# Which rows of x a chunk takes: runs of 1 KB against runs of 6 to 7 KB, and a strided read in VectorE's transposes

## The reference

```python
mask = adj > 0
head = mask.astype(adj.dtype)
head = head / jnp.maximum(jnp.sqrt(jnp.sum(head * head, axis=-1, keepdims=True)), 1e-12)
inc = adj + head                      # each positive entry gains 1 / sqrt(count of positives in its row)
edge_fea = inc @ x
edge_degree = jnp.sum(inc, axis=-1, keepdims=True)
out = layernorm(x + edge_fea / edge_degree)
```

## Time and profile before

| | us |
|---|---|
| median of 3 runs | 430.42 |
| lowest and highest | 429.62, 434.88 |
| the execution that was profiled | 431.71 |
| its span, first to last instruction | 429.9 |
| TensorE busy (matmuls) | 396.9 |
| VectorE busy | 371.7 |
| GpSimd busy | 351.1 |
| ScalarE busy | 346.5 |

### The profile page before, as it was taken

The page is one execution under the profiler, slowest core; times in us unless marked ns, Lnnn a source line. Parts: engine busy times, 40 slices in busy tenths (PEclk is TensorE's granted clock), DMA queues, the critical chain, the costliest instruction groups (busy, mean ns, idle before and its releaser), DMA issues.

```text
span 429.9 us, 8836 instructions
## 1 busy us (share of the span) xinstructions
PE 396.9 (92%) x2152; PEld 344.8 (80%) x2152; DVE 371.7 (86%) x739; ACT 346.5 (81%) x450; POOL 351.1 (82%) x266
## 2 busy tenths in 40 slices
PE   1199767999999999999999999999999999999995
PEld 0177646888888888888888888888888888888884
DVE  0859489899999999999999999999999999999932
ACT  5766799888899889898889988888988999896200
POOL 3108069899999999999999999999999999999850
PEclk9999888999999999999999999999999999999999
DMA  8999857666656666766666666676666666660010
GB/s 233 270 240 263 242 147 220 199 189 194 197 186 199 187 202 207 220 199 192 196 187 196 191 194 197 205 219 202 192 195 194 189 196 189 196 205 24 26 38 12
DMA packets 38219, 79.85 MB, mean 186 GB/s; under 512 B 9536, under 2 KB 21824, under 8 KB 38208
## 3 DMA queue, kind: packets, MB, share of 16 engines
q1 hardware_dynamic: 37824, 78.68, 62.4%
q10 hardware_dynamic: 384, 1.05, 0.8%
HBM read 75.50 MB, written 4.19 MB: 185 GB/s over the span
## 4 chain that ended last, share of the span: by engine, by line
PE 84%; SPq 5%; issue 4%; POOL 2%; DMA 2%; DVE 1%; POOLq 0%
PE edge L618 41%; PE edge L577 21%; PE edge L621 21%; SPq L187 3%; SPq L157 2%; DMA x_stage<-in_x_dram 2%; POOL inc_split L344 2%; PE sums L572 1%; SPq L182 0%; POOL inc_split L349 0%; DVE incT L436 0%; POOL rstd L328 0%; POOLq L45 0%; DVE rows L463 0%; DVE rows L467 0%
## 5 line engine op out<-in xcount | busy, mean ns | idle before, releaser
L618 PE MATMUL edge<-x_split,inc_split 128*128 128x512 f32 (+1 forms) x810 | 281.4, 396 | 0.1
L344 POOL TENSOR_TENSOR inc_split<-incT,inc_split 128x832 fp32r<-128x832 f32 x120 | 237.2, 1987 | 10.5 <-DVE incT L436 7.6
L621 PE MATMUL edge<-x_split,inc_split 128*128 128x256 f32 x780 | 218.3, 280 | 0.0
L618 PEld LDWEIGHTS edge<-x_split,inc_split 128*128 128x128 f32 x810 | 152.9, 189 | 34.9 <-POOL inc_split L344 0.6
L220 ACT ACTIVATE sign_out<-raw,sign_bias 128x1024 bf16<-128x1024 f32 x128 | 146.4, 1144 | 32.4 <-DMA raw<-in_adj_dram 30.9
L420 DVE SCALAR_TENSOR_TENSOR inc<-raw,scaled 128x1024 f32<-128x1024 f32 x128 | 153.5, 1199 | 5.4 <-ACT scaled L231 5.4
L436 DVE STREAM_TRANSPOSE incT<-inc 128x1024 f32<-128x1024 f32 x128 | 155.4, 1225 | 0.2
L231 ACT ACTIVATE scaled<-raw,norm 128x1024 f32<-128x1024 f32 x128 | 141.7, 1108 | 13.1 <-DVE inc L420 6.6
L621 PEld LDWEIGHTS edge<-x_split,inc_split 128*128 128x128 f32 x780 | 147.7, 189 | 0.0
L577 PE MATMUL edge<-x_native,incT 128*128 128x256 f32 x384 | 96.6, 390 | 7.3 <-DVE incT L436 7.3
L577 PEld LDWEIGHTS edge<-x_native,incT 128*128 128x128 f32 x384 | 69.0, 192 | 16.4 <-DVE incT L436 8.1
(11 more groups left out here) (36 smaller groups left out, 104.9 us busy)
## 6 DMA issues: line engine op xcount, KB each, us to landing
raw<-in_adj_dram SPq DMA_DIRECT2D x504, 128.0 KB, 2.6
rows<-in_x_dram SPq DMA_DIRECT2D x32, 128.0 KB, 2.1
out_dram<-rows SPq DMA_DIRECT2D x32, 128.0 KB, 1.7
x_stage<-in_x_dram SPq DMA_DIRECT2D x8, 224.0 KB, 9.5
x_stage<-in_x_dram SPq DMA_DIRECT2D x8, 192.0 KB, 9.7
raw<-in_adj_dram ACTq DMA_DIRECT2D x8, 128.0 KB, 5.4
x_native<-in_x_dram SPq DMA_DIRECT2D x4, 192.0 KB, 7.3
```

The lines of the kernel that those rows point to most:

```text
L344: nc.gpsimd.tensor_tensor(lo_of(s, q), incT[:, s, 0:SPLIT, q, :], hi_of(s, q).bitcast(fp32), ALU.subtract).then_inc(lo_by_pool, 1)
L618: nc.tensor.matmul(edge[s][:, c0:c1], inc_split[s][:, 0, b, :, :].rearrange("p q j -> p (q j)"), x_split[:, b, :, :].rearrange("p h d -> p ...
L621: last = nc.tensor.matmul(edge[s][:, D:2 * D], inc_split[s][:, 1, b, :, :].rearrange("p q j -> p (q j)"), x_split[:, b, 0, :], start=False ...
```

## The change

Chunk b of x is now made of other rows. Before, partition j of a quadrant held row 32 b + j of the quadrant's 1024; now it holds row 32 j + b. So what a partition needs for several chunks lies in one piece in memory. The sum over the 1024 columns of a quadrant is the same, in another order, as long as `incT` has its columns in the same places; so the transposes read `inc` for block b not at 32 b, 32 b + 1, ... but at b, b + 32, b + 64, ... The output of the transposes, all shapes, the number of instructions and DMAs, and all waits stay as they are.

```diff
-    x_v = x.rearrange("(g b j) d -> g j b d", g=G, j=SQ)
+    x_v = x.rearrange("(g j b) d -> g j b d", g=G, j=SQ)
...
                 dve.wait_ge(inc_ready, G * t + q + 1)
                 nc.vector.transpose(incT[:, s, :, q, :],
-                                    inc[:, q, :].rearrange("p (b j) -> p b j", j=SQ)).then_inc(incT_ready, 1)
+                                    inc[:, q, :].rearrange("p (j b) -> p b j", j=SQ)).then_inc(incT_ready, 1)
```

## The result

The changed kernel takes 499.56 us (median of 4 runs, 499.43 to 500.47); the kernel before, measured beside it, 431.12 us. The ratio is 1.156, with a 95% interval of 1.151 to 1.161: 68 us slower. The prediction was 545 us in a range of 426 to 600, with 0.65 on slower by over 2%. So wide a range would have held almost any price of a transpose; the distance from 545, 45 us, says more.

What follows compares the result with a forecast made beforehand. TensorE was taken as the bound, VectorE close behind and becoming it once transposes lengthen. Start 49.28 + 5.6, tiles 337.3 + 128.4 + 1.7 and tail 21.95 gave 544.3 us of span, 545 us of time; range 426 to 600.

Steps and rivals of the forecast that it cites:

- The margin of VectorE: In each flat tile VectorE waits 0.7 us for TensorE; each of four transposes may grow 0.16 us before VectorE bounds.
- d: What one transpose gains in length; forecast 1.07 us, from 0.65 to 1.44 with chance 0.52.
- end to end: Above 0.16 us per transpose, VectorE's work is simply laid in sequence; a tile period under 11.2 + 4d would contradict it.
- The price of a transpose: Each of 128 transposes on VectorE takes one more step for each lone word: +1.07 us, 2.30 us in all.
- The upper bound from L396: L396's mean of 2.61 ns per element, reading two SBUF words, caps a transpose at 2.67 us, 1.44 more.
- The sum: Start, tiles 2 to 31 and tail added along VectorE: 407.8 + 128 d, giving 545 us.
- The faster x: From 20 to 36 us, x in longer runs moves at 286 GB/s instead of 239, winning 2.6 us.
- the free read: Rival: strided transpose reads cost nothing, TensorE stays the bound, x lands 2.6 us sooner; 427.8 us, chance 0.30.
- The last rival: Longer runs of x bring nothing, the memory's side limiting DMA; with a free read 430.4 us; inside that rival's 0.30.
- That the start reaches the end: A microsecond won or lost before tile 2's first inc at 49.28 us is one at the end.
- the cap of 2.94 us: Most that faster x can win at the start: the wait of tile 2's count behind VectorE's low halves of x.
- TensorE's clock: Could make a second bound in the tiles; even with 3 us at 1.2 GHz TensorE needs 13.4 of 15.5 us.

Runs made afterwards that it cites:

- e4_runs: Kernel before, with transposes reading in order in quarter 0, pairs in quarter 1, fours in quarter 2, lone words 32 apart in quarter 3; 434.17 us.
- e3_strides: Kernel before, with transposes reading at a stride of 2 words in quarter 0, then 4, 8 and 16 in the others; 482.87 us.
- e1_x_only: Kernel before with only the new rows of x, transposes still reading in order; 432.16 us against 433.13, ratio 1.000.
- e7_pairs_of_rows: Kernel before with two rows of x in one run and all transposes at a stride of 2 words; 432.77 us against 432.74, ratio 0.999.
- e10_less_x: Kernel before without the last of the four parts of x_stage, its readers reading the third again; 429.11 us against 432.64, ratio 0.993.

## Why the prediction was right or wrong, point by point

- **The margin of VectorE.** Right in kind: one tile leaves it some 0.6 us, in the end some 0.8, and beyond that its work is laid end to end. `e4_runs` (434.17 us at d = 0.22) and `e3_strides` (482.87 us at d = 0.64) stand on both sides of the edge. The prediction's own sign against "end to end" did show: the period of 14.27 us is shorter than 11.2 + 4d = 14.5. But VectorE is busy in all of it; what got shorter is two small steps (below, the sum).
- **The price of a transpose** is the term that was mis-sized: +1.07 us assumed, +0.82 measured. At 128 transposes this is 32 of the 45 us between 545 and 500. I took a whole VectorE step for each word, because one step seemed the natural size; the extra cost of a lone word is (1.93 - 1.23)/1,024 = 0.69 ns, two thirds of the 1.05 ns of a step, with some 0.15 us more for a transpose beside a busy TensorE. What made me side with so high a price was the row of L396, and that row says nothing of one (next point). That a price was there was right, then, but not by this argument: it was in part luck. The Trainium skill (Vector Engine (DVE) Microarchitecture Reference, Measured stream behaviour on trn2) gives 1.73 ns for each column of an instruction with two sources, one of which hops 4 KiB at every element; its 2.50 ns is for both sources, or the destination alone, stepping by 24 words, and not for one source, as the prediction reads it. With the 152 ns of the earlier trace rows, 1.73 ns makes 1.92 us for a transpose, an estimate, and the trace has 1.89 to 1.96 where TensorE stands still. That is close for another instruction and another distance; the 1.98 to 2.26 us at strides of 4, 8 and 16 words show that one figure doesn't cover all. By its 497 us the kernel would have been forecast almost to the point, though partly by offset: the Trainium skill's figure leaves out TensorE's company, and my sum was too high elsewhere.
- **The upper bound from L396** held as a number, but is no bound of this price. The Trainium skill (SBUF — State Buffer, Who interferes with whom) says that a VectorE instruction with two inputs in SBUF contends with GpSimd's reads. The profile agrees. These are the second L396 and the GpSimd instruction beside it before, then L396 after (least, median, greatest) and the last GpSimd instruction beside it:

```profile
38.25 5.55 DVE L396 TENSOR_TENSOR x_split<-x_stage,x_split 128x1536 fp32r<-128x1536 f32 x1
...
36.65 5.53 POOL L355 TENSOR_TENSOR x_split<-x_stage,x_split 128x1792 fp32r<-128x1792 f32 x1
...
L396 DVE TENSOR_TENSOR x_split<-x_stage,x_split x2: 1746/2963/4180, 41.2 to 45.3; 128x1536 fp32r<-128x1536 f32 x2
...
39.81 4.00 POOL L355 TENSOR_TENSOR x_split<-x_stage,x_split 128x1792 fp32r<-128x1792 f32 x1
```

  Before, GpSimd ends at 42.18 us and L396 at 43.80, 1.6 us behind it. After, GpSimd ends at 43.81 and the first L396, begun at 41.24, at 45.42, again 1.6 us behind it; the second one, with GpSimd idle, takes 1.75 us. That is 1.14 ns for each element, about one step, with two words from SBUF for each. So the second word costs nothing here, and what made L396 long was GpSimd. The prediction also read the company wrongly: GpSimd did not run beside the 5,546 ns instance throughout, but left it 1.6 us before its end, and it was busy beside all of the 2,466 ns one.
- **The sum.** With d = 0.82 it gives 407.8 + 105.0 = 512.8 us, 13 more than measured. At the start it has +3.6 us and the trace +0.26: L396 got 2.1 us shorter, and the chain of tile 0 had begun 0.3 us sooner. In the middle, from the first inc of tile 2 to the end of the last transpose, it has 337.3 + 98.4 + 1.7 = 437.4 us and the trace 477.60 - 49.54 = 428.1. Of these 9.3 us, L489 makes 5.6 (21.8 to 16.2 us busy) and L464 1.1; I had carried both over at their old lengths. L489 goes with GpSimd too: in the tiles it ends some 0.15 us behind the GpSimd instruction that it begins beside, in both kernels, and that one has about 0.49 us left to run before and 0.36 after; with GpSimd idle it takes 0.41 us. In the tail the sum has 21.95 us and the trace 497.8 - 477.6 = 20.2. The step from the span to the time gives 1.3 us back: I added 0.5 us, and the execution has 1.8.
- **The faster x.** Wrong as a price, without effect on the forecast, in which VectorE hid it. It would have mattered in the rival of the free read, whose 427.8 us was in truth 432 (`e1_x_only`, `e7_pairs_of_rows`). The failed step is "I take the second rate for the first stretch": two stretches that differ in the length of their runs differed in more than that. The last rival, that longer runs bring nothing, was the right one here for the time, though its reason, a limit on the memory's side, isn't shown.
- **That the start reaches the end, and the cap of 2.94 us**: both right (`e10_less_x`).
- **TensorE's clock** as a second bound: it did fall, to 0.95 to 0.97 on average between 100 and 400 us, and TensorE's busy time rose to 12.1 to 13.9 us a tile, but stayed under 14.27. From 49.54 us to the tail VectorE waited once for it, 1.4 us for the signs' sums, and never for its products.
- **The free read**, 0.30: false at 32 words, true at 2. I had weighed the jumps of the output, once in 32 words, and called them too rare to tell; `e4_runs` shows that on the side of the read even one jump for every two words is free, so jumps that rare told nothing.

## What to carry to other kernels

Before a layout is changed so that DMA runs get longer, ask which engine then reads in lone words, and how much room it has: here 4 x 0.82 us fell on an engine with 0.6 us to spare, 32 times. A transpose's read was free at a stride of 2 words, so the mild form (two rows in a run, a stride of 2) can be had for nothing. A price read off an instruction with two inputs is worth nothing before one has looked at what GpSimd did beside it. And a difference in rate between two stretches isn't the worth of the one feature by which one means to explain it; a kernel with that feature alone tells for the price of one run.

## What the runs showed of the hardware that was not expected

- A transpose of 128 x 1024 float32 on VectorE takes, in the median, 1.22 us at strides of 1 and 2 words, 2.02 at 4, 2.26 at 8, 1.98 at 16, and at 32 from 1.89 to 2.16. Runs of 2 or 4 neighbours with jumps of 64 or 128 words between them take 1.23 and 1.21.
- TensorE's products slow VectorE's transposes of lone words from 1.89 to 1.96 us up to 1.97 to 2.16, and leave those that read in order at 1.25 or less.
- A VectorE instruction with two inputs in SBUF (L396) took 1.75 us with GpSimd idle, and beside GpSimd's L355 it ended 1.6 us after that one, whenever it had begun: up to 5.55 us in all.
- The loads of x_stage move at 232 to 246 GB/s from 24 to 34 us in runs of 1, 2, 4 and 7 KB and from either tensor, and at 241 to 249 where they come later in the queue; the adj of tile 2 and 3 behind them moves at 256 to 295 from 38 to 46 us. The longer runs lower the engines' share from 1.13 to 1.01. The cause stays open.
